# Decoder layers: the scores of a cross attention computed for eight heads at a time on two 64-row halves of the array

## The reference

```python
Q = proj(query, Wq, bq)            # 8 x 16 heads x 256 tokens x 16
K = proj(key, Wk, bk)              # 8 x 16 heads x  77 positions x 16
V = proj(value, Wv, bv)
scores = jnp.einsum('bhqd,bhkd->bhqk', Q, K) / np.sqrt(D_K)
scores = jnp.where(m == 0, NEG, scores)      # second layer: scores + mask
attn = jax.nn.softmax(scores, axis=-1)
x = jnp.einsum('bhqk,bhkd->bhqd', attn, V)
return x.transpose(0, 2, 1, 3).reshape(b, -1, D_MODEL) @ Wo.T + bo
```

## Time and profile before

| | us |
|---|---|
| median of three runs | 1294.27 |
| the profiled execution, whole time | 1291.09 |
| its span in the trace | 1289.3 |
| TensorE busy | 1087.8 (84% of the span) |
| VectorE busy | 961.6 (75%) |
| ScalarE busy | 704.9 (55%) |
| GpSimd busy | 388.9 (30%) |

### The profile page before, as it was taken

One profiled execution on the slowest core, in us unless ns is written; L12 is line 12 of the kernel. 1 busy time (PEld: TensorE's weight loads), 2 busy tenths in 40 slices (PEclk: granted clock), 3 DMA queues, 4 the chain that ended last, 5 costly groups with the idle time before them and its releaser, 6 DMA issues. The chain is left out here.

```text
span 1289.3 us, 30260 instructions
## 1 busy us (share of the span) xinstructions
PE 1087.8 (84%) x10763; PEld 881.4 (68%) x10763; DVE 961.6 (75%) x2254; ACT 704.9 (55%) x1459; POOL 388.9 (30%) x538
## 2 busy tenths in 40 slices
PE   4899989999987699986269999389999569999696
PEld 3578878778776577774257777378787447777485
DVE  7587877878875488884938883569998538888497
ACT  2454444444443355552637775368788525655484
POOL 5122222222220355551130000423331225555232
PEclk9899999999999799995559999699999879999799
DMA  6000000100000500005245431300000000000011
GB/s 257 5 10 2 10 12 2 71 3 2 2 2 2 187 23 22 11 9 227 107 135 172 171 108 49 120 17 26 24 9 9 0 24 23 11 21 9 34 50 50
DMA packets 34072, 65.35 MB, mean 51 GB/s; under 512 B 7590, under 2 KB 23334, under 8 KB 30886
## 3 DMA queue, kind: packets, MB, share of 16 engines
q1 hardware_dynamic: 32422, 59.62, 13.2%
q0 software_dynamic: 1536, 4.20, 1.0%
HBM read 43.03 MB, written 12.39 MB: 43 GB/s over the span
## 5 line engine op out<-in xcount | busy, mean ns | idle before, releaser
L953 POOL TENSOR_TENSOR ca_z<-ca_z,ca_top 128x308 f32<-128x308 f32 x128 | 92.7, 724 | 129.8 <-DVE ca_top L1082 129.5
L389 ACT ACTIVATE wa_probs<-wa_scores,wa_minus_top 128x192 f32<-128x192 f32 x256 | 83.3, 437 | 80.6 <-DVE wa_minus_top L477 80.6
L1025 ACT ACTIVATE ca_pth<-ca_turned 77x512 f16<-77x512 f32 x128 | 75.9, 593 | 59.0 <-PE ca_turned L1209 58.4
L348 POOL TENSOR_TENSOR wa_q<-wa_by_cos,wa_by_sin 128x256 f32<-128x256 f32 x32 | 23.4, 732 | 266.3 <-DVE wa_by_sin L472 266.3
L1209 PE MATMUL ca_turned<-ident,ca_probs 128*77 128x128 f32 x512 | 84.1, 287 | 20.6 <-ACT ca_probs L1017 19.5
L400 ACT ACTIVATE wa_pth<-wa_turned 128x384 f16<-128x384 f32 x128 | 58.4, 506 | 73.5 <-PE wa_turned L696 73.5
L1200 PE MATMUL ca_scores<-ca_km,ca_q 128*128 128x308 f32 x256 | 89.6, 433 | 6.0 <-ACT ca_q L998 5.7
L1087 DVE SCALAR_TENSOR_TENSOR ca_ptl<-ca_turned,ca_pth 77x512 f16<-77x512 f32 x128 | 86.7, 677 | 2.6 <-ACT ca_pth L1025 2.6
L1017 ACT ACTIVATE ca_probs<-ca_z 128x308 f32<-128x308 f32 x128 | 58.2, 455 | 44.8 <-POOL ca_z L953 43.8
L621 PE MATMUL wa_scores<-wa_xh,wa_wh 128*128 128x256 f16 x256 | 70.5, 275 | 11.7 <-DVE wa_wl L456 9.7
L477 DVE TENSOR_REDUCE wa_minus_top<-wa_scores 128x2 f32<-128x384 f32 x128 | 62.3, 549 | 21.1 <-PE wa_scores L684 18.9
(11 more groups left out here) (332 smaller groups left out, 3677.0 us busy)
## 6 DMA issues: line engine op xcount, KB each, us to landing
ex_stage<-in_ew SPq DMA_DIRECT2D x16, 1024.0 KB, 7.0
slots<-slots_zeros SPq DMA_DIRECT2D x10, 512.0 KB, 5.3
ca_xs<-tokens SPq DMA_DIRECT2D x16, 256.0 KB, 2.3
ex_xe<-slots SPq DMA_DIRECT2D x11, 320.0 KB, 3.3
slots<-ex_y SPq DMA_DIRECT2D x9, 320.0 KB
wa_x_stage<-in_xt SPq DMA_DIRECT2D x8, 256.0 KB, 3.0
tokens<-in_x SPq DMA_DIRECT2D x1, 2048.0 KB, 14.8
ca_w<-in_xw SPq DMA_DIRECT2D x2, 1024.0 KB, 5.6
```

Of the source, the lines that this page charges most:

```text
L389: ins = act.activation(probs[2 * (u % 2) + t][:, h, t * WINDOW:t * WINDOW + SPAN], s_bank[i][:, t * SPAN:(t + 1) * SPAN], ACT.Exp, bias=mi ...
L953: pool.tensor_tensor(z[k][:], z[k][:], top[:, k].unsqueeze(2).broadcast_to((P, UH, CTX)), ALU.subtract).then_inc(shift, 1)
L1025: act.activation(pth[k][0:CTX], t_bank[k][0:CTX], ACT.Copy, scale=PSCALE).then_inc(probs_high, 1)
```

## The change

Heads 0 to 3 of a group of eight lie on rows 0 to 63 of the query and key, heads 4 to 7 on rows 64 to 127. The scores of two units, a pair, are now two matmuls on 64 rows each: one on the upper half into one PSUM bank, one on the lower half into the neighbouring bank. The pair is issued at the end of units 1, 3, 5 and 7, for the units c + 3 and c + 4. The two banks hold one pair, so a pair's matmuls wait until VectorE has masked the pair before. Mask and maximum take eight heads in one instruction each, in even units, and `z` doubles in size; subtraction and exponential still go by four heads. In the ring the tokens move to slot 2 and the query to slot 4, and slot 5 is empty. Normalising, the application of the norm and the value's low part move within VectorE's units.

```diff
@@ -772,17 +772,19 @@
 CTX = 77
 CH, CD = 16, 16
 UH = 4
+HALF = UH * CD
 UNITS = TPB * CH // UH
+PAIRS = UNITS // 2
 MASKED = -4.0e9
 OPEN = 1.0e38
 CA = Ring(
     steps=[
         [("key", 0)],
         [("value", 0)],
-        [("heads", 1)],
+        [("heads", 1), ("tokens", 0)],
         [("mix", 1)],
-        [("tokens", 0)],
         [("query", 0)],
+        [],
         [("heads", 0)],
         [("mix", 0)],
     ],
...
@@ -847,7 +849,7 @@
         xb = sb("xb", [P, TPB, DIM])
 
         shared = [ctx.enter_context(nc.psum_tensor(f"{tag}_shared{k}", [P, 512], F32)) for k in range(2)]
-        s_bank = [ctx.enter_context(nc.psum_tensor(f"{tag}_scores{k}", [P, 512], F32)) for k in range(2)]
+        s_banks = ctx.enter_context(nc.psum_tensor(f"{tag}_scores", [P, 2 * UH, P], F32))
         t_bank = [ctx.enter_context(nc.psum_tensor(f"{tag}_turned{k}", [P, 512], F32)) for k in range(2)]
         o_bank = [ctx.enter_context(nc.psum_tensor(f"{tag}_out{k}", [P, CH, 32], F32)) for k in range(2)]
...
@@ -1064,12 +1067,12 @@
 
             def mask_scores(b, c):
 
-                k = c % 2
-                dve.wait_ge(scores, b * UNITS + c + 1)
-                if not (first(b) and c < 2):
-                    dve.wait_ge(exped, b * UNITS + c - 1)
-                s = s_bank[k][:, 0:UH * CTX].rearrange("p (h k) -> p h k", h=UH)
-                m = at(mask if additive else limit, b * TPB + c // (UNITS // TPB)).unsqueeze(1).broadcast_to((P, UH, CTX))
+                k = c // 2 % 2
+                dve.wait_ge(scores, b * PAIRS + c // 2 + 1)
+                if not (first(b) and c < 4):
+                    dve.wait_ge(exped, b * UNITS + c - 2)
+                s = s_banks[:, :, 0:CTX]
+                m = at(mask if additive else limit, b * TPB + c // (UNITS // TPB)).unsqueeze(1).broadcast_to((P, 2 * UH, CTX))
                 if additive:
                     ins = dve.scalar_tensor_tensor(out=z[k][:], in0=s, scalar=CD ** -0.5, in1=m, op0=ALU.mult, op1=ALU.add)
                 else:
@@ -1077,8 +1080,8 @@
                 ins.then_inc(masked, 1)
 
             def take_maximum(b, c):
-                k = c % 2
-                dve.wait_ge(masked, b * UNITS + c + 1)
+                k = c // 2 % 2
+                dve.wait_ge(masked, b * PAIRS + c // 2 + 1)
                 dve.tensor_reduce(top[:, k], z[k][:], AX.X, ALU.max).then_inc(maxed, 1)
 
             def probs_rest(b, c):
@@ -1108,25 +1111,23 @@
             def batch(b, par, before=True, after=True):
                 for c in range(UNITS):
                     two_on = (b, c + 2) if c < UNITS - 2 else (b + 1, c + 2 - UNITS) if after else None
-                    if two_on:
+                    if two_on and c % 2 == 0:
                         mask_scores(*two_on)
-                    probs_rest(b, c)
-                    if two_on:
                         take_maximum(*two_on)
                     if c == 5:
                         normalise(b, 0)
                     if c == 1 and before:
                         normalise(b - 1, 1)
+                        norm.apply(dve, b - 1, 0, at(X, (b - 1) * TPB))
+                    probs_rest(b, c)
                     for kind, i, bank, uses in CA.slot(c, b):
                         if kind == "value":
                             value(b + 1, 1 - par, bank, uses)
                         if kind == "mix":
                             residual(b + CA.serves(kind, i), i, bank, uses)
-                    if c == 0 and before:
-                        norm.apply(dve, b - 1, 0, at(X, (b - 1) * TPB))
                     if c == 5 and before:
                         norm.apply(dve, b - 1, 1, at(X, (b - 1) * TPB + 1))
-                    if c == 2 and after:
+                    if c == 3 and after:
                         value_low(b + 1, 1 - par)
 
             for kind, i, bank, uses in CA.prologue():
...
@@ -1189,16 +1189,20 @@
                         ins = pe.matmul(dst[:, 0:DIM], ot[:, i, g], w[:, 3, g], start=(g == 0), stop=(g == KT_ - 1))
                 ins.then_inc(full[bank], 1)
 
-            def score(b, c, par):
+            def score_pair(b, c, par):
+
                 t, part = divmod(c, UNITS // TPB)
-                g, h = part // 2, UH * (part % 2)
+                g = part // 2
                 if c == 0:
                     wait_read(pe, [("query", 0)], b)
                     pe.wait_ge(key_masked, (b + 1) * KT_)
-                if not (first(b) and c < 2):
-                    pe.wait_ge(masked, b * UNITS + c - 1)
-                pe.matmul(s_bank[c % 2][:, 0:UH * CTX], q[par][:, g, t * P:(t + 1) * P],
-                          km[par][:, g, h:h + UH].rearrange("p h k -> p (h k)"), start=True, stop=True).then_inc(scores, 1)
+                if not (first(b) and c == 0):
+                    pe.wait_ge(masked, b * PAIRS + c // 2)
+                for k in range(2):
+                    rows = slice(HALF * k, HALF * (k + 1))
+                    ins = pe.matmul(s_banks[:, UH * k:UH * (k + 1), 0:CTX], q[par][rows, g, t * P:(t + 1) * P],
+                                    km[par][rows, g, UH * k:UH * (k + 1)], start=True, stop=True)
+                ins.then_inc(scores, 1)
 
             def turn_probs(b, c):
                 k = c % 2
@@ -1227,10 +1231,6 @@
             def batch(b, par, before=True, after=True):
                 for c in range(UNITS):
                     turn_probs(b, c)
-                    if c < UNITS - 2:
-                        score(b, c + 2, par)
-                    elif after:
-                        score(b + 1, c + 2 - UNITS, 1 - par)
                     for kind, i, bank, uses in CA.slot(c, b):
                         d = CA.serves(kind, i)
                         step(b + d, (par + d) % 2, kind, i, bank, uses)
@@ -1238,12 +1238,16 @@
                         weigh(b, c - 1, par)
                     elif before:
                         weigh(b - 1, UNITS - 1, 1 - par)
+                    if c in (1, 3):
+                        score_pair(b, c + 3, par)
+                    if c in (5, 7) and after:
+                        score_pair(b + 1, c - 5, 1 - par)
```

22 lines of the change are left out of this document (11 added, 11 removed).

## The result

The kernel after was timed beside the kernel before in three groups of runs, each on one chip:

| group | before, median | after, median | ratio, 95% interval | mean granted clock of after's runs |
|---|---|---|---|---|
| first | 1295.50 (4 runs) | 1287.15 (4) | 0.9941 [0.9919, 0.9963] | 0.9145 |
| second (after_again) | 1296.24 (13) | 1284.24 (6) | 0.9899 [0.9881, 0.9917] | 0.9188 |
| third (after_third) | 1294.02 (11) | 1283.55 (6) | 0.9924 [0.9903, 0.9945] | 0.9215 |

What follows compares the result with a forecast made beforehand. TensorE and VectorE, both near full, plus waits were taken to bound the kernel. Fourteen batches, each 1.0 us shorter (18.29 to 17.3), save 14 us: profiled execution 1291.09 to 1277, median 1294.27 to 1280 us; range 1265 to 1300.

Steps and rivals of the forecast that it cites:

- The price of a pair: On TensorE, two score matmuls on 64 rows each cost 0.84 us, 0.74 from their start to the transposes behind.
- no overlap: Rival: a pair's two halves on TensorE do not overlap at all; 1.36 us per pair, time 1309; chance 0.08.
- half an overlap: Rival: of a half's two records only the second runs beside the other half; 1.10 us per pair, 1295; chance 0.17.
- no edges: Rival: 64-row tiles on TensorE cost no edges; 0.52 us per pair, 28 us less, time 1266; chance 0.13.
- VectorE's instructions: Mask and maximum of eight heads cost 0.72 and 0.71 us; 0.15 saved per pair, 0.6 per batch.
- The batch: One middle batch of a cross attention, laid out by hand: 16.68 + 0.55 = 17.2, taken as 17.3 us against 18.29.
- 0.55 wait of unit 5: In unit 5, TensorE's weighting wants VectorE's low part of unit 4 at 7.17 and gets it at 7.72.
- A late link: Rival: ScalarE's full unit 2 or the low part behind the pair holds TensorE 0.6 us longer; batch 17.9, 1289; chance 0.12.
- for what the hand misses: Allowance on the hand-laid batch: its sum of 17.2 us was taken as 17.3.
- the late query: In unit 6 the next batch's scores waited for the new query; claimed root of 1.6 us of waits per batch.
- The sum: Seven batches in each cross attention, 14 x 1.0 = 14 us less; start and last batch counted at nothing.
- The start: At each cross attention's start the first subtraction comes 0.64 us later; the last batch gives about as much back.

Runs made afterwards that it cites:

- e_full_rows: Kernel after, with each pair's two score matmuls on all 128 rows and not on 64; 1292.23 us, ratio 0.9951.
- e_between4: Kernel after, with the maximum of the pair in unit 4 put behind the low part; 1286.74 us, ratio 0.9943.
- e_ring_only: Kernel before with the new ring table alone (tokens in slot 2, query in slot 4, slot 5 empty); 1298.32 us, ratio 1.0006.
- e_idle_both: Kernel after, with unread 240-column matmuls where TensorE is idle in the first and last batch of each cross attention; 1279.16 us, ratio 0.9864.
- e_twice: Kernel after, with each pair of score matmuls issued twice in a row; 1304.34 us, ratio 1.0055.
- e_split4: Kernel after, with unit 4's maximum split: heads 0 to 3, the low part, then heads 4 to 7; 1284.45 us, ratio 0.9926.
- e_split4_late: e_split4 with the second tile's norm (line 159) applied in unit 6 behind the maximum, not in unit 5; 1279.30 us, ratio 0.9888.

## Why the prediction was right or wrong

- **The price of a pair** was right: 0.72 to the transposes against 0.74, and its split into work and edges too (0.51 for two more halves). The rivals "no overlap" (1.26) and "half an overlap" (1.0) are out, so is "no edges". The rule of the Trainium skill that a change of tiling mode drains the engine (TensorEngine Tiling (Array Packing), Key Properties) agrees with the cost beyond work, 0.72 and a gap of 0.10 ahead less 0.51, about 0.3, of which e_full_rows leaves 0.27 to the halves. The prediction read the strict order of matmuls (TensorE: Matmul & The Clock Gate, The mechanism, in the Trainium skill) as a case for 1.0 us. The order is kept and the pair still takes 0.72: its four records start at 501.817, 501.824, 502.181 and 502.187 and end in that order (502.34, 502.35, 502.60, 502.61), two and two side by side. What failed in that rival, as far as these records show, is its picture that the second record of one half goes ahead of the first of the other.
- **VectorE's instructions**: 0.82 and 0.71 start to start against 0.72 and 0.71. The mask is 0.10 dearer ahead of the maximum, which reads its result; ahead of the low part, in e_between4, it is 0.71.
- **The batch**: 17.40 against 17.3, with the 0.55 wait of unit 5 where it was put (0.47). "A late link" as a rival (17.9) is out. That the mean comes so near is in part luck: batches without a loop start take 17.15, by hand 17.2, and the 0.1 added "for what the hand misses" stands for a wait behind the loop's start of 0.3 to 0.6 in every second batch, which no step of the prediction has.
- **Where a batch's gain comes from** was put wrongly. I said that pairs save TensorE nothing on the path, and that the gain lies in waits with the late query as their root. e_ring_only removes the late query and gains nothing; e_full_rows keeps the order and the ring and loses 0.69 of the 0.96. The order puts all score work into the heavy units, where each 0.2 counts; with full rows the same hand schedule gives 17.3 + 4 x 0.2 = 18.1, and 18.09 was measured, though by three times 0.26 and not by four times 0.2. The schedule was right, the reason told beside it was not.
- **The sum** failed, in the step "there are seven such batches in each cross attention" together with "I count both at nothing" for start and last batch. Forecast were 12 us from twelve middle batches, 2 from the two first ones and 0 from the ends. Measured in the profiled executions, cut at the transposes: 11.4 from the middle, 0.0 from the first batches, -0.9 at the starts and -1.9 in the tails, 8.6 of 14. The first batch gains only where the clock lets it: 1.4 in the first cross attention, where before had a half-clock stretch there too, and -1.4 in the second, where it had none; at full clock it would have been 1.1 (see e_idle_both), as the prediction has it. In the tail, the seven units from the transposes of unit 0 to those of unit 7 take 14.11 after and 14.09 before in the first cross attention, so nothing is given back; in the second, 15.26 and 14.10, with 3.88 for a unit 3 that takes 2.46 in after_again without the half clock. "I am also wrong if the granted clock in these stretches leaves 1.00" was written for the middle batches, where it stayed; I did not look at the ends with it.
- **The start**: from the first pair to the first transposes of the second cross attention 3.79 us (1049.94 to 1053.73) against 3.14 before, 0.65 more, forecast 0.64. It is given back nowhere.
- **A slip in a rival**: with the price at 0.52 the prediction's own units add up to about 15.8, not 16.0. Nothing hangs on it.

So of the 14 us that were forecast 8.4, 10.5 and 12.0 were measured; the medians, 1284 to 1287, lie inside the range of 1265 to 1300.

## What to carry to other kernels

Work a steady loop out by hand, but count its passes from the trace, and give the first and the last pass a sum of their own, with their own granted clock: less work on TensorE in a pass with gaps may cost the full clock there. The first batch, cut at the transposes, took 17.9 to 18.8 us in six cross attentions of after, and 17.3, 17.7 and twice 18.0 with more score work in the same order (e_full_rows, e_twice). When a link that a schedule puts at 0.5 us is taken away and nothing is gained, look for an instruction whose duration, not whose start, has changed: it may have slid onto another engine's access. Before crediting one part of a change, take each part out of the new kernel and also put it alone into the old one: the ring was worth +0.2 alone and -1.4 within.

## What the runs showed of the hardware that was not expected

- VectorE's tensor-scalar instruction (line 159, 128 x 256 float32, from SBUF to SBUF) takes 0.40 us alone and 0.95 or 0.66 when it starts early in a tensor-tensor instruction of GpSimd; it ended 0.15 us behind GpSimd's in both (502.06 after 501.91 in e_split4, 505.54 after 505.39 in e_between4). Where it starts in the last 0.2 us of one, it keeps its 0.40. The other way round, GpSimd's subtraction takes 0.80 and not 0.70 when it starts during that instruction (503.25 in e_split4_late). The Trainium skill (SBUF — State Buffer, Who interferes with whom) says that such an instruction of VectorE and one of GpSimd exclude each other over a shared port pair, and that the later one waits for the whole of the first. These rows agree: the same 0.15 behind two different starts speaks for a wait to the end. No wait is shown for it in the timeline; only the duration grows.
- The time of one and the same kernel follows its granted clock: 0.73 us per 0.001 over 61 runs, from 1288.5 to 1301.5 us. Two kernels compared over few runs can differ by several us for that alone.
- Two float32 matmuls of 308 columns on two halves of the rows, into neighbouring banks, take 0.51 us beside each other (two more halves in e_twice), as long as one on all rows (0.52 in the earlier trace rows). The first two of a pair's four records start 7 ns apart.
